# Three cross attentions of a four-layer Perceiver: order of loads, unrolled heads, a split last head, three score banks and keys in three pieces

## The reference

```python
# second layer (L1)
q = (hidden_states @ Wq.T + bq) * scaling      # k, v = ctx @ W.T + b, split into 16 heads
scores = jnp.einsum('bhtd,bhsd->bhts', q, k) + bias      # bias: 1 x 16 x 128 x 12544
probs = jax.nn.softmax(scores, axis=-1)
attn = jnp.einsum('bhts,bhsd->bhtd', probs, v)
attn = attn.reshape(B, T, E)                   # heads are not transposed back
return attn @ Wo.T + bo
# fourth layer (L3)
scores = jnp.einsum('bnlh,bnph->bnlp', qm, km) / np.sqrt(HEAD_DIM)
scores = jnp.where(mask, scores, MASK_FILL)    # MASK_FILL = -1e8
out = jnp.einsum('bnlp,bnph->bnlh', jax.nn.softmax(scores, axis=-1), vm)
return out.transpose(0, 2, 1, 3).reshape(B, L, D_MODEL) @ Wo.T + bo
```

## Time and profile before

| | us |
|---|---|
| median of 3 runs | 3043.82 (3042.2 to 3044.83) |
| the profiled execution | 3044.07 |
| its span | 3042.3 |
| second layer's cross attention, from its first load | 980.3 to 1461.7 |
| fourth layer's cross attention | 2498.6 to 2881.9 |

### The profile page before, as it was taken

One profiled execution on the slowest core, in us unless ns is written; L12 is line 12 of the kernel. 1 busy time (PEld: TensorE's weight loads), 2 busy tenths in 40 slices (PEclk: granted clock), 3 DMA queues, 4 the chain that ended last, 5 costly groups with the idle time before them and its releaser, 6 DMA issues. The chain is left out here.

```text
span 3042.3 us, 67057 instructions
## 1 busy us (share of the span) xinstructions
PE 2813.4 (92%) x24065; PEld 1856.6 (61%) x24065; DVE 1784.0 (59%) x3582; ACT 1511.7 (50%) x2408; POOL 718.8 (24%) x388
## 2 busy tenths in 40 slices
PE   7999999998978799999899999999998788999988
PEld 5555555554757466666456666666666574666678
DVE  3222323322253777786648888888888528888532
ACT  2333233332331588888236666666665333656521
POOL 2332231221000000000006666666665000000000
PEclk9999999999999799999899999999998798999979
DMA  7888878787815999996622222222222383555455
GB/s 219 282 270 252 258 250 254 254 258 229 274 36 192 419 381 385 381 385 243 213 104 68 66 64 66 67 64 66 64 67 68 119 244 100 151 151 147 116 198 186
DMA packets 329007, 578.74 MB, mean 190 GB/s; under 512 B 78641, under 2 KB 264833, under 8 KB 321665
## 3 DMA queue, kind: packets, MB, share of 16 engines
q1 hardware_dynamic: 328857, 576.59, 57.3%
HBM read 395.49 MB, written 181.05 MB: 190 GB/s over the span
## 5 line engine op out<-in xcount | busy, mean ns | idle before, releaser
L1668 POOL TENSOR_TENSOR l2x_sums<-l2x_sums,all_S 128x768 f32<-128x768 f32 (+1 forms) x195 | 474.6, 2434 | 189.4 <-ACT all_S L1992 182.6
L1872 DVE TENSOR_TENSOR all_S<-all_S,l2x_minus 128x1024 f32<-128x1024 f32 x224 | 381.7, 1705 | 1.9 <-ACT l2x_minus L1988 1.9
L1709 PE MATMUL l2x_key_bank<-ahead_ctx,early_nat_out 128*64 128x512 f32 (+1 forms) x1536 | 323.1, 541 | 0.0
L648 PE MATMUL prep_work<-prep_wv,prep_ctxT 128*128 128x512 f32 x688 | 300.3, 594 | 0.1
L1853 DVE TENSOR_TENSOR l2x_tops<-l2x_scores,l2x_tops 128x768 f32<-128x768 f32 (+1 forms) x208 | 223.5, 1074 | 117.8 <-PE l2x_scores L1725 117.8
L1268 DVE TENSOR_REDUCE l3x_rowmax<-l3x_scores 128x1 f32<-128x448 f32 x448 | 263.4, 622 | 39.7 <-PE l3x_scores L1188 38.2
L1343 ACT ACTIVATE l3x_pT<-l3x_turned 128x896 f32<-128x896 f32 x224 | 205.0, 917 | 163.4 <-PE l3x_turned L1196 160.1
L1992 ACT ACTIVATE all_S<-all_S 128x1024 f32<-128x1024 f32 x224 | 213.4, 953 | 97.3 <-DVE all_S L1872 97.3
L1099 ACT ACTIVATE all_S<-all_S,l1x_negmax 128x896 f32<-128x896 f32 x224 | 233.2, 1044 | 48.4 <-DVE l1x_negmax L1045 32.5
L958 PE MATMUL l1x_turned<-all_ident,all_S 128*128 128x128 f32 x1568 | 220.6, 282 | 20.0 <-ACT l1x_pT L1020 13.3
L1740 PE MATMUL l2x_out<-all_S,l2x_values 128*64 128x128 f32 x3136 | 226.2, 285 | 10.9 <-ACT all_S L1992 10.8
(11 more groups left out here) (676 smaller groups left out, 4472.2 us busy)
## 6 DMA issues: line engine op xcount, KB each, us to landing
l1x_bias<-in_fside_Bx16xSxS_dram SPq DMA_DIRECT2D x112, 896.0 KB, 6.8
scratch_k<-prep_kparts SPq DMA_DIRECT2D x84, 672.0 KB, 3.3
l1x_k_half<-scratch_k SPq DMA_DIRECT2D x32, 1568.0 KB, 9.9
keys_k<-scratch_k SPq DMA_DIRECT2D x32, 1176.0 KB, 7.3
l2x_values<-scratch_v SPq DMA_DIRECT2D x112, 256.0 KB, 2.6
scratch_k<-prep_kparts SPq DMA_DIRECT2D x56, 448.0 KB, 4.8
scratch_v<-prep_st_v SPq DMA_DIRECT2D x11, 2048.0 KB, 9.2
scratch_v<-prep_st_v SPq DMA_DIRECT2D x14, 1536.0 KB, 7.2
```

The source lines that it names most:

```text
L648: last = nc.tensor.matmul(w[:, h, :], ctxT[:, k, j * P:(j + 1) * P], wv2[:, k, h * 512:(h + 1) * 512], start=(k == 0), stop=(k == KT - 1))
L1668: nc.gpsimd.tensor_tensor(sums[odd][:, 0:n], sums[odd][:, 0:n], in_memory(u), ALU.add).then_inc(added, 1)
L1709: last = nc.tensor.matmul(keys_ps[u % 2][half * VW:(half + 1) * VW, 0:n], wk_cur[odd][:, k, :], ahead.piece[u // 2][:, k, c:c + n], start= ...
L1872: nc.vector.tensor_tensor(part, part, minus[:, :].unsqueeze(1).to_broadcast([P, blocks_of(u), P]), ALU.add).then_inc(shifted, 1)
```

## The change

Six things, each in one of the two streams:

1. Second layer, first loads: a new order for the transfers of heads 0 and 1 (`load_first_head`).
2. Second layer, ScalarE: the 16 heads are written out, without the loop of four passes.
3. Second layer, sum and division: `sum_tiles` of head h stands behind turn 1 of head h + 1, the division before slot 3. Head 0 stands ahead of the loops on TensorE and VectorE.
4. Second layer, last head: VectorE copies all groups but 2, 5, 8 and 11.
5. Second layer, end: 15 heads get their bias, are stored and read back into `att_rows` during the last head, and are transposed behind its last `weigh`. The last head's 16 columns are divided and biased in one instruction, spread over 128 x 256 by a product with a 0/1 pattern, and two matmuls with `row_of` sum them into the last 8 columns of each transposed block.
6. Fourth layer: a third score bank (the PSUM tile that held sum and turned maximum, which move), `weigh` in pairs of groups, keys in three pieces (0 to 3584, to 6272, to 12544) with a semaphore each.

```diff
+        by_last = by if heads == 1 else ["s" if c % 3 == 2 else "v" for c in range(GRP)]
...
+    def load_first_head(sp):
+        load_keys(sp, 0, 0, True)
+        for i in range(3):
+            load_bias(sp, 0, i, True)
+        load_keys(sp, 0, 1, True)
+        for i in range(3, GRP // 2):
+            load_bias(sp, 0, i, True)
+        load_keys(sp, 1, 0, False)
...
+        for i in range(3, GRP // 2):
+            load_bias(sp, 1, i, False)
+        load_keys(sp, 1, 1, False)
...
     def tensor_head(...):
+            if tiles > 1 and c == 1 and not first:
+                sum_tiles(pe, h - 1)
+        if beside is not None:
+            beside(pe)
-        if tiles > 1:
+        if tiles > 1 and not following:
             sum_tiles(pe, h)
...
     def vector_head(...):
+            if tiles > 1 and c == 3 and not first:
+                dve.wait_ge(summed, h)
+                divide(dve, h - 1, sum_ps)
+                if beside is not None:
+                    beside(dve)
...
     def on_scalar(act):
-            turn = 4
-            with act.Fori(0, heads // turn) as g:
-                for j in range(turn):
-                    scalar_head(act, g * turn + j)
+        for h in range(heads):
+            scalar_head(act, h)
...
-    scores_ps = [ph.ps(f"scores{i}", [P, 512]) for i in range(2)]
+    scores_ps = [ph.ps(f"scores{i}", [P, 512]) for i in range(2)] + [sum_ps]
...
+                load_k(i * 2 + s + 2, s, 0)
+                load_k(i * 2 + s + 2, s, 1)
+                load_v(i * 2 + s + 1, 0)
+                load_k(i * 2 + s + 2, s, 2)
+                load_v(i * 2 + s + 1, 1)
...
-            if c >= lag:
+            if c > lag and (c - lag) % 2 == 1:
+                weigh(pe, h, c - lag - 1)
                 weigh(pe, h, c - lag)
...
+                    def add_stored(dve):
+                        dve.wait_ge(run.out_taken, HEADS)
+                        dve.wait_ge(loaded, 32)
+                        nc.vector.tensor_tensor(att[:, 0:D - 16], ..., ALU.add).then_inc(att_ready, 1)
+                    def divide_last(dve, product, inverse, taken):
+                        nc.vector.scalar_tensor_tensor(att[:, D - 16:D], product[:, 0:16], inverse[:, 0:1],
+                                                       bb["bv"][:, D - 16:D], op0=ALU.mult, op1=ALU.add)
+                    nc.vector.tensor_tensor(last_spread, att[:, D - 16:D] ..., place_of ..., ALU.mult)
```

More of the change, by code:

```diff
@@ L869, in head_stream, with copier, copies_done @@
     n_by = {e: by.count(e) for e in "vs"}
-    rank = [by[:c + 1].count(by[c]) for c in range(GRP)]
+    by_last = by if heads == 1 else ["s" if c % 3 == 2 else "v" for c in range(GRP)]
+    def copier(h, c):
+        return by_last[c] if isinstance(h, int) and h == heads - 1 else by[c]
+    def copies_done(h, c):
+        order = by_last if isinstance(h, int) and h == heads - 1 else by
+        return (h + 1) * n_by[order[c]] + order[:c + 1].count(order[c])
     more_scores = scores_ps is not None
@@ L1085, in on_vector @@
         if heads > 1:
-            with dve.Fori(0, heads - 1) as h:
+            vector_head(dve, 0, True, first=True)
+            with dve.Fori(1, heads - 1) as h:
                 vector_head(dve, h, True)
-        vector_head(dve, heads - 1, False)
+        vector_head(dve, heads - 1, False, first=heads == 1, beside=beside)
+        if tiles > 1:
+            dve.wait_ge(summed, heads)
+            divide_last(dve, sum_ps, inverse, out_taken)
         dve.wait_ge(out_taken, heads + 1)
@@ L1160, in on_sync, with load_k @@
         sp.sem_inc(parts_ready, 1)
-        def load_k(h, s, j):
-            hold(sp, held, turned_full, (h - 2) * GRP + GRP // 2 * (j + 1))
-            keys.load_k(sp, h, s, j)
+        def load_k(h, s, i):
+            hold(sp, held, turned_full, (h - 2) * GRP + keys.pieces[i][1] // GW)
+            keys.load_k(sp, h, s, i)
         def load_v(h, j):
@@ L1182, in scores @@
         j, at = b // GRP, b % GRP
-        if at == 0:
-            pe.wait_ge(k_loaded[s][j], (h // 2 + 1 if isinstance(h, int) else h[0] + 1) * 16 * N_K)
+        for i, (first_key, _) in enumerate(keys.pieces):
+            if b * HB == first_key:
+                pe.wait_ge(k_loaded[s][i], (h // 2 + 1 if isinstance(h, int) else h[0] + 1) * 16 * N_K)
         hh = h if isinstance(h, int) else h[0] * 2 + h[1]
-        pe.wait_ge(scores_taken, hh * NB + b + 1)
-        nc.tensor.matmul(scores_ps[b % 2][:, 0:HB], q[:, bass.ds(hh * P, P)],
+        if b >= 3:
+            pe.wait_ge(scores_taken, hh * NB + b - 2)
+        elif not (isinstance(hh, int) and hh == 0):
+            if b == 0:
+                pe.wait_ge(scores_taken, hh * NB)
+            elif b == 1:
+                pe.wait_ge(q_ready, hh)
+        nc.tensor.matmul(scores_ps[b % 3][:, 0:HB], q[:, bass.ds(hh * P, P)],
                          kt[s][j][:, at * HB:(at + 1) * HB], start=True, stop=True).then_inc(scores_full, 1)
@@ L1206, in weigh @@
             pe.wait_ge(parts_ready, h + 1)
+            if not (isinstance(h, int) and h == 0):
+                pe.wait_ge(out_taken, h)
         pe.wait_ge(exp_done, h * GRP + c + 1 + 2)
```

130 lines of the change are left out of this document (85 added, 45 removed).

## The result

The changed kernel took 3009.59 us (median of 4 runs, 3003.66 to 3012.91) against 3043.01 us (4 runs, 3035.58 to 3044.83): ratio 0.9893, 95% interval 0.988 to 0.9907. Forecast were 3023.5 us and a range of 3011 to 3033; the time lies 1.4 us under the range. The profiled execution took 3011.99 us, its span is 3010.3.

What follows compares the result with a forecast made beforehand. Second layer's heads were taken as set by ScalarE, then TensorE, with the data queue full; the fourth layer's by TensorE. Terms summed to -20.5 us from 3044.07, so 3023.5 us, range 3011 to 3033.

Steps and rivals of the forecast that it cites:

- first loads: Second layer's start: row maximum 7.8 us sooner, but a 7 us stop for head 1's second key half and half clock; net +1.8 us.
- table loads: Second layer, ScalarE: one exponential table load in place of four saves three of 1.28 us, -3.85 us.
- sum put off: Second layer: sum and division moved into the next head start its first turn 0.9 us earlier, but nothing follows: 0.
- the end, with the output matmul: Second layer's end: shorter path behind the last weighing, -5.2 us, and output matmul no longer at half clock, -0.9 us.
- next stage: Stage behind the second layer's cross attention: its first steps -0.5 us, with ends 0 and -2.5.
- fourth layer: 15 heads: Fourth layer's steady heads: paired weighings save 0.44 us per head, -6.6 us; ends 0 and -1.0 per head.
- Rival A: Second layer: putting the sum off shortens every head, -12 us more, 3011.5 us; chance 0.12.
- Rival B: Second layer's start: head 1's second key half does not bind, so -7.8 in place of +1.8, 3014 us; chance 0.08.
- C: Second layer, ScalarE: the page's drain is real and goes with the table load, 3 x 1.38 us more, 3019.4 us; chance 0.05.
- D: Fourth layer: VectorE bounds the steady head, so banks and pairs change nothing there, 3030 us; chance 0.12.
- E: Second layer: ScalarE's straight code for 16 heads must be fetched and holds it, +36 us, 3059.5 us; chance 0.07.
- term of 0 for key pieces: Fourth layer: the cut brings the first key piece earlier, the last about 1 us later: 0, with 1.5 us of slack.

## Why the prediction was wrong

| step | forecast | measured |
|---|---|---|
| first loads | +1.8 | +3.0 |
| table loads | -3.85 | -4.5 with what follows a load |
| sum put off | 0 | 0 |
| last head's copies | -2.4 | -2.3 |
| the end, with the output matmul | -6.1 | -6.1 |
| next stage | -0.5 | -2.8 |
| fourth layer: start | -2.6 | -2.1 |
| fourth layer: 15 heads | -6.6 | -17.5 |
| fourth layer: tail | -0.3 | -0.6 |

Of the 4.5 us in the row of the table loads, 4.4 are accounted for: 3 x 1.28 for the loads, 3 x 0.08 for the heads behind them and 0.33 for head 1, which took 27.07 us with ScalarE's loop (27.10 before) and 26.77 without.

**The step that failed is the fourth layer's steady head**, "I take 0.44 per head x 15". Its sign was right and its mechanism was seen in part; the size was off by nearly three: 17.5 us against 6.6, beyond my own end of -1.0 per head as well. I priced the pairs by one changeover, "0.09 x 7 = 0.6 per head if TensorE bounds", the longer score ahead of a weighing. The rows hold more: two weighings apart take 2 x 0.55 us of TensorE's time, 28 matmuls in a row 0.98 (2673.24 to 2674.22), another 0.12. So a pair saves 0.24 in the two slots (2.86 to 2.62), and I had 0.09. Then I shaded even this, since early in the head VectorE bound; that was in the main the two banks' coupling (TensorE's waits for maxima in 250 us fell from 6.4 to 2.3 us). The parts by the runs: third bank 0.35 per head once the division is out of its way, pairs 1.1 on top of it; 7 x 0.24 would be 1.7, and why it is less is open. Taken one by one from the rows of before, each seemed small, and each alone measured as nothing: the bank brought a wait of its own (the division) that the pairs hid, the pairs brought a wait (two banks) that the third bank hid. A sum of separate terms cannot show that.

**The next stage** became 2.8 us shorter where I had 0.5, just beyond the end I had set (-2.5). The 13.3 us from the stage's start, before and after:

```profile
1461.70:1475.00 13.30, 10.85 (x43) 7.63 (x44) 8.03 (x106) 3.11 (x5) 0.00 (x0) 0.54 0.83 304
```

```profile
1453.70:1467.00 13.30, 12.78 (x49) 8.54 (x50) 8.03 (x106) 3.87 (x7) 0.00 (x0) 0.68 0.87 307
```

In both, TensorE is at clock 0.50 until its value matmuls begin, and these begin 8.81 us behind the stage's start before and 6.76 after:

```profile
1470.51 5.80 PE L2933 MATMUL l1a_value<-l1a_wv,early_ctx 128*128 128x512 f32 x9 [1.92 <-DMA l1a_wv<-in_L_xattn_Wv_dram]
```

```profile
1460.46 8.03 PE L3027 MATMUL l1a_value<-l1a_wv,early_ctx 128*128 128x512 f32 x16
```

So 2.0 of the 2.8 us go with a wait for a transfer that was 1.92 us before and nil after, and the rest, as far as the windows show, with the clock, which rises sooner. The variants say that the new end of the second layer's attention is behind it: from that transfer's issue to the last of the first 64 value matmuls the four profiled kernels with the old end take 36.7 to 37.2 us, the twelve with the new end 33.5 to 34.6. They don't say by which way, since some kernels with the new end wait for the transfer too, up to 1.5 us, and have the clock up sooner instead.

**Right, and by the reasons given.** The first loads: the row maximum came at 1011.27, the key half of head 1 stopped TensorE for 7.26 us (forecast 7) with half clock behind it (0.50 to 1038, 0.74 in the next 2 us), and the sign was a loss. It landed 51.8 us after the first load (50.4 before), and that makes most of the 1.2 us by which the loss was larger. The rows that the term's clock part took from before hold three groups of seven transposes at half clock, not "seven turns"; the 5.9 us are right. Rival A fell: heads without a load are 26.80 with the sum put off or not. The time landed beside its 3011.5, by another cause. Rival B fell with the stop, C and D with the heads' lengths. E fell: from head 1 on none is longer than 26.81 with straight code. The last head and the end came out within 0.2 us.

**The term of 0 for key pieces** was right for the cut, as far as one execution of each can tell, but "1.5 us of slack as cover" was used up from both sides. The heads became 1.4 us shorter, and the transfer longer; the key transfers of 1176 KB from 2550 to 2800 us (number, size, median us from issue to landing), before and after:

```profile
keys_k<-scratch_k SPq DMA_DIRECT2D x23, 1176.0 KB, 7.2
```

```profile
keys_k<-scratch_k SPq DMA_DIRECT2D x12, 1176.0 KB, 9.1
```

With three pieces and weighings one at a time it was 7.4, so the cut did not lengthen it. Against the kernel with four pieces, the stops cost 0.35 us a head in the profiled execution, 5 us in all, and from nothing to 0.7 us a head in others.

The rest of the difference, +1.9 us ahead of the second layer and -1.1 in its experts and the third layer, is left open; what the code does there is the same in both.

## What to carry to other kernels

Price a part of a change in the schedule it will stand in, not in the old one: two edits that each remove the other's new wait can be worth nothing singly and 1.4 us a head together. Where TensorE goes from one kind of matmul to another, read the start-to-start times across the change in both directions, not the durations alone; and ask whether TensorE bounds there, since the same pairing gave nothing where ScalarE did. When a queue is full, reordering moves the wait to whatever stands last, and a head made shorter can use up the slack of the transfers beside it.

## What was not expected of the hardware

- 28 value matmuls in a row took 0.98 us start to next, 14 twice 1.10 us; a score ahead of them 0.29, ahead of turned keys 0.20. Changing over between kinds costs in both directions.
- ScalarE's loop set a load at each pass, 1.28 us, and the head behind it was 0.08 us longer too; straight code behind the loop had no load.
- The landing of a key half of the same size varied from head to head at a DMA share of 0.61: in the profiled execution of the changed kernel 6 of 15 heads were 0.3 to 2.4 us longer than the rest, with halves 2 heads by 2.8 and 3.2. It varied from execution to execution too: with the same fourth layer the mean head was 20.34 us in one and 20.98 in another.
